# Spreading the first norm's means by DMA and subtracting them on GpSimd

## What is computed

```python
def _ln_c(v, eps=1e-06):
    m = jnp.mean(v, axis=1, keepdims=True)
    s = jnp.var(v, axis=1, keepdims=True)
    return (v - m) / jnp.sqrt(s + eps)
...
x = x + conv_ref(_ln_c(x), ...)
t = _to_tokens(x)
t = t + ffn_ref(_ln_t(t), ...)
```

## Time and profile before

| | |
|---|---|
| median of three runs | 628.01 us (627.54 to 630.71) |
| profiled execution | span 630.2 us from first to last instruction; no own time is given beside it, and of the three runs only 630.71 is not below the span |
| mean granted clock of PE | 0.916 |
| PE busy | 541.1 us, 86% of the span |
| DVE busy | 487.1 us, 77% |
| ACT busy | 436.5 us, 69% |
| POOL busy | 188.7 us, 30% |
| DMA | 73.38 MB, mean 116 GB/s |

### The profile page before, as it was taken

How to read it: one execution, slowest core, us unless ns; L and a number is a source line. 1 busy time by engine, 2 the same in 40 slices (tenths; PEclk the granted TensorE clock), 3 DMA queues, 4 the chain that set the end, 5 groups by cost and what they waited for, 6 DMA issues and landing times.

```text
span 630.2 us, 14170 instructions
## 1 busy us (share of the span) xinstructions
PE 541.1 (86%) x5732; PEld 274.7 (44%) x5732; DVE 487.1 (77%) x950; ACT 436.5 (69%) x651; POOL 188.7 (30%) x116
## 2 busy tenths in 40 slices
PE   3659999998989898998999899989898988977982
PEld 1333444444444444444444444434443433344762
DVE  5575565789888978897899779987888798799520
ACT  2455788787977796779767976897687855974110
POOL 1008362115302440235022602080308044130045
PEclk9956998999999989998999799989998999976595
DMA  8960245623661457144714453435411265520000
GB/s 193 196 152 14 101 129 158 170 80 91 189 179 62 109 156 190 57 136 134 200 70 135 133 157 113 136 101 167 134 43 61 91 182 152 160 81 5 6 16 19
DMA packets 26752, 73.38 MB, mean 116 GB/s; under 512 B 4152, under 2 KB 4152, under 8 KB 22592
## 3 DMA queue, kind: packets, MB, share of 16 engines
q1 hardware_dynamic: 25664, 71.44, 41.2%
q0 software_dynamic: 1024, 1.05, 0.6%
HBM read 38.40 MB, written 34.08 MB: 115 GB/s over the span
## 4 chain that ended last, share of the span: by engine, by line
PE 44%; DVE 28%; ACT 12%; issue 11%; DMA 2%; another core or an unknown queue 1%; POOL 0%; SPq 0%; ACTq 0%; DVEq 0%; POOLq 0%
PE st L372 10%; PE cv L383 8%; PE bc L494 6%; PE tl L400 6%; PE cv L391 5%; DVE us L949 5%; ACT junk L810 5%; DVE xs L959 5%; DVE lg L947 3%; PE tl L409 3%; DVE cnd L1041 2%; DVE top_i L1046 2%; ACT tok L775 2%; DVE us L951 2%; DMA xs<-in_x 2%
## 5 line engine op out<-in xcount | busy, mean ns | idle before, releaser
L1437 POOL TENSOR_TENSOR xs<-xs,us 128x1024 f32<-128x1024 f32 x64 | 150.7, 2376 | 360.3 <-DVE xs L959 177.4
L959 DVE SCALAR_TENSOR_TENSOR xs<-cv,vecs,xs 128x1024 f32<-128x1024 f32 x64 | 82.0, 1282 | 25.2 <-PE cv L391 24.9
L770 ACT ACTIVATE hid<-cv,b1n 128x1024 f32<-128x1024 f32 x64 | 71.3, 1115 | 39.3 <-PE cv L383 38.8
L803 ACT ACTIVATE sqc<-us 128x1024 f32<-128x1024 f32 x64 | 67.6, 1056 | 42.3 <-DVE us L949 41.6
L400 PEld LDWEIGHTS tl<-ident,xs 128*128 128x128 f32 x512 | 64.4, 196 | 56.9 <-issue 56.9
L951 DVE CUSTOM_DVE_ANT_0 us<-us,bc 128x1024 f32<-128x1024 f32 x60 | 73.0, 1216 | 19.0 <-PE bc L494 17.7
L949 DVE TENSOR_TENSOR us<-xs,bc 128x1024 f32<-128x1024 f32 x60 | 73.0, 1216 | 17.5 <-PE bc L494 17.1
L810 ACT ACTIVATE junk<-us 128x1024 bf16<-128x1024 f32 x64 | 67.5, 1055 | 20.5 <-DVE gsum L951 19.9
L372 PE MATMUL st<-xs,stat_w 128*32 128x256 f32 x1024 | 72.6, 404 | 8.9 <-DMA xs<-in_x 8.9
L400 PE MATMUL tl<-ident,xs 128*128 128x128 f32 x512 | 77.1, 296 | 1.6 <-ACT lg L785 1.6
L409 PE MATMUL tl<-xs,gcen 128*32 128x256 f32 x1024 | 71.7, 400 | 7.4 <-ACT tok L775 7.4
(11 more groups left out here) (210 smaller groups left out, 657.0 us busy)
## 6 DMA issues: line engine op xcount, KB each, us to landing
xs<-in_x SPq DMA_DIRECT2D x64, 512.0 KB, 7.0
out_rows<-tok SPq DMA_DIRECT2D x64, 512.0 KB
us<-in_e_w SPq DMA_DIRECT2D x8, 260.0 KB
xs<-in_e_w SPq DMA_DIRECT2D x8, 256.0 KB
sqc<-out_rows,idx_all POOLq DMA_INDIRECT x16
out_rows<-sqc,idx_all POOLq DMA_INDIRECT x16
vecs<-in_b SPq DMA_DIRECT2D x4, 0.2 KB, 14.0
gate_bias<-in_gate_b SPq DMA_DIRECT2D x4, 0.1 KB, 12.4
```

The source lines that it names most:

```text
L959: nc.vector.scalar_tensor_tensor(out=xu, in0=cv[:], scalar=vecs[:, 3:4], in1=xu, op0=ALU.add, op1=ALU.add).then_inc(x1_done, 1)
L1437: nc.gpsimd.tensor_tensor(xu, xu, su, ALU.add).then_inc(s_done, 1)
```

## The change

For batches 2 to 7 the first norm's mean is no longer spread by PE. DVE copies the sums of part i (pairs 0 and 1, pair 2, pair 3) into `mean_f` (which is the buffer `ta`), SP writes them to a DRAM tensor `means` in DMAs of two rows of 256 (16, 8 and 8 of them), waits until they have landed, and loads each half pair's means back into `us`, one row of 8 KB for all of 64 partitions (4, 2 and 2 DMAs). POOL then computes x - mean (centre). `xs` becomes one ring of nine pairs, so the loads move: pair 0 in step 0 of batch n - 2, pairs 1, 2, 3 in its steps 3, 5, 7. x_sums of pairs 0, 1, 2 stand in steps 4, 5, 6, of pair 3 in step 0 of the next. The squares of two units move into the batch before (`NEXT_SQUARES`), `sqc` has four units instead of three, the last square sums and ln1_rsqrt and rstd are in step 3, S jobs begin at (3, 2) and the third and fourth L job are at (2, 1) and (2, 2). In the tail, `ew2` and `eq` use the last four pairs of the ring, and the DMA scratch space is set to 4096 bytes. The core of the diff:

```diff
...
@@ -36,7 +36,8 @@
 RING = 6
 CAND = PIECES * K
 MRG = 2 * CAND + PIECES
-SQC = 3
+SQC = 4
+SLOTS = 9
...
 C_JOBS = {(0, 0): 0, (0, 1): 1, (0, 2): 2, (1, 0): 3, (2, 0): 4, (2, 1): 5, (2, 2): 6, (3, 0): 7}
-S_JOBS = {(4, 0): 0, (4, 1): 1, (4, 2): 2, (5, 0): 3, (5, 1): 4, (5, 2): 5, (6, 0): 6, (6, 1): 7}
-L_JOBS = {(1, 1): 0, (1, 2): 1, (3, 1): 2, (3, 2): 3}
+FIRST_S_JOBS = {(4, 0): 0, (4, 1): 1, (4, 2): 2, (5, 0): 3, (5, 1): 4, (5, 2): 5, (6, 0): 6, (6, 1): 7}
+S_JOBS = {(3, 2): 0, (4, 0): 1, (4, 1): 2, (4, 2): 3, (5, 0): 4, (5, 1): 5, (6, 0): 6, (6, 1): 7}
+L_JOBS = {(1, 1): 0, (1, 2): 1, (2, 1): 2, (2, 2): 3}
+LAST_L_JOBS = {(1, 1): 0, (1, 2): 1, (3, 1): 2, (3, 2): 3}
+FIRST_SQUARES = {(s, i): k for (s, i), k in C_JOBS.items()}
+SQUARES = {(0, 0): 2, (0, 1): 3, (1, 1): 4, (1, 2): 5, (2, 1): 6, (2, 2): 7}
+NEXT_SQUARES = {(7, 1): 0, (7, 2): 1}
 E_JOBS = {(7, 0): 0, (7, 2): 1}
...
     p1, tl = it + 1 < NB, 1 <= it <= NB
     jobs = {}
+    if p1 and it <= 0:
+        jobs.update({at: ("C", k) for at, k in C_JOBS.items()})
     if p1:
-        jobs.update({at: ("C", k) for at, k in C_JOBS.items()})
-        jobs.update({at: ("S", k) for at, k in S_JOBS.items()})
+        jobs.update({at: ("S", k) for at, k in (S_JOBS if it >= 1 else FIRST_S_JOBS).items()})
     if tl:
         jobs[LAST_M_JOB if it == NB - 1 else M_JOB] = ("M", it - 1)
         if it < NB:
-            jobs.update({at: ("L", k) for at, k in L_JOBS.items()})
+            jobs.update({at: ("L", k) for at, k in (L_JOBS if p1 else LAST_L_JOBS).items()})
     if it == NB - 1:
         jobs.update({at: ("E", k) for at, k in E_JOBS.items()})
     if it == NB:
...
+    return k // 2 + 1 if n == 0 else NG + k // 4 + 1
+def mean_part_count(n, i):
+    return NG + 2 + 3 * (n - 2) + i + 1
+def squares_at(it, at):
+    if it <= 0:
+        return [(it + 1, k) for k in [FIRST_SQUARES.get(at)] if k is not None] + (
+            [(it + 2, k) for k in [NEXT_SQUARES.get(at)] if k is not None] if it == 0 else [])
+    return ([(it + 1, SQUARES[at])] if it + 1 < NB and at in SQUARES else []) + (
+        [(it + 2, NEXT_SQUARES[at])] if it + 2 < NB and at in NEXT_SQUARES else [])
 def mk_metaformer_kernel(nc, x, gn_w, gn_b, w1T, b1, w2T, b2, gateT, gate_b, e_w1, e_w2, e_b2, *outs):
...
         us = [sb(f"us{i}", [P, HW]) for i in range(2)]
         lg = sb("lg", [P, RING * PIECE])
...
+        def x_col(n, u):
+            return UN * (2 * ((NG * n + u // 2) % SLOTS) + u % 2)
+        def x_unit(n, u):
+            return xs[:, x_col(n, u):x_col(n, u) + UN]
...
-            def load(b, m, slot):
+            def load(b, m):
+                col = x_col(b, 2 * m)
                 for h in range(HALVES):
-                    sp.dma_start(xs[slot][C * h:C * h + C, 2 * UN * m:2 * UN * (m + 1)], x_h[b, h, :, m, :]).then_inc(x_in[m], 16)
+                    sp.dma_start(xs[C * h:C * h + C, col:col + 2 * UN], x_h[b, h, :, m, :]).then_inc(x_in[m], 16)
+            def spread_means(n, i):
+                m0, m1 = ((0, 2), (2, 3), (3, 4))[i]
+                sp.wait_ge(mean_ready, mean_part_count(n, i))
+                if n >= 4:
+                    for m in range(m0, m1):
+                        sp.wait_ge(mean_in[m], 32 * (n - 3))
+                for c in range(4):
+                    src = mean_f[32 * c + 4 * m0:32 * c + 4 * m1, :]
+                    for m in range(m0, m1):
+                        for sub in range(2):
+                            q = 4 * (m - m0) + 2 * sub
+                            sp.dma_start(means[n % 2, m, :, c, sub, :], src[q:q + 2, :]).then_inc(mean_out, 16)
+                sp.wait_ge(mean_out, 16 * 8 * (NG * (n - 2) + m1))
+                sp.wait_ge(c_done, NU * (n - 2) + 2 * m1)
+                sp.wait_ge(s_done, NU * (n - 2) + 2 * m1)
+                for m in range(m0, m1):
+                    for h in range(HALVES):
+                        row = means[n % 2, m, h].rearrange("c s r -> (c s r)").unsqueeze(0).broadcast_to([C, 2 * UN])
+                        sp.dma_start(us[n % 2][C * h:C * h + C, 2 * UN * m:2 * UN * (m + 1)], row).then_inc(mean_in[m], 16)
...
                 sp.wait_ge(sumx_done, m + 1)
-                load(1, m, 1)
+                load(1, m)
+            sp.wait_ge(sumx_done, mean_count(1, 0))
+            load(2, 0)
             def load_weights(part):
...
             def step(it, s):
-                par, (b, u) = it % 2, (it, s - 1) if s else (it - 1, NU - 1)
+                (b, u) = (it, s - 1) if s else (it - 1, NU - 1)
+                if s == 1 and it >= 1 and it + 1 < NB:
+                    spread_means(it + 1, 2)
+                if s in (6, 7) and it + 2 < NB:
+                    spread_means(it + 2, s - 6)
                 if b >= 0:
                     store(b, u)
                 if it == NB - 1:
                     load_weights(s)
-                if s == 0 and b >= 0 and it + 1 < NB:
+                if s == 0 and b >= 0 and it + 2 < NB:
                     sp.wait_ge(grp_done, NG * it)
                     sp.wait_ge(e_done, NU * it)
-                    load(it + 1, NG - 1, 1 - par)
+                    load(it + 2, 0)
                 if it + 2 < NB and s >= 3 and s % 2 == 1:
                     sp.wait_ge(grp_done, NG * it + (s - 3) // 2 + 1)
-                    load(it + 2, (s - 3) // 2, par)
+                    load(it + 2, (s - 3) // 2 + 1)
...
-                mm = sum_group(st1[:, 0:SUB], xs[n % 2], m, NU, True)
-                if m % 2 == 1:
+                if n >= 2 and m >= 2:
+                    pe.wait_ge(mean_ready, mean_part_count(n, m - 2))
+                mm = sum_group(st1[:, 0:SUB], xs, m, x_col(n, 2 * m), True)
+                if (m >= 1) if n >= 2 else (m % 2 == 1):
                     mm.then_inc(sumx_done, 1)
             def first_x_sums(m):
                 pe.wait_ge(x_in[m], 32)
                 wait(pe, mean_ready, m)
-                sum_group(st2[:, 0:SUB], xs[0], m, NU, True).then_inc(sumx_done, 1)
...
                 if s == 0 and b >= 0:
                     x1_sums(b, b % 2, NG - 1)
-                if s == 1 and p1:
-                    xc_square_sums(n, 0)
-                if s == 2 and p1:
-                    xc_square_sums(n, 1)
+                if s in (1, 2) and it == 0:
+                    xc_square_sums(n, s - 1)
                 if s == 4:
                     x1_sums(it, par, 1)
                 if s in (3, 7):
...
-                if s in (0, 1) and p1:
+                if s in (0, 1) and it == 0:
                     x_sums(n, s + 2)
-                if s == 3 and p1:
+                if s == 0 and it >= 1 and p1:
+                    x_sums(n, 3)
+                if s == 1 and it >= 1 and p1:
+                    pe.wait_ge(mean_ready, mean_part_count(n, 2))
+                    xc_square_sums(n, 0)
+                    xc_square_sums(n, 1)
+                if s == 2 and it >= 1 and p1:
+                    xc_square_sums(n, 2)
+                if s == 3 and it == 0:
                     xc_square_sums(n, 3)
-                if s in (4, 6) and n + 1 < NB:
-                    x_sums(n + 1, s // 2 - 2)
+                if s in (4, 5, 6) and n + 1 < NB:
+                    x_sums(n + 1, s - 4)
                 if s == 4 and n + 1 >= NB:
...
+            def square_xc(n, k):
+                if n < 2:
+                    used(act, n - 1, "C", k)
+                else:
+                    act.wait_ge(xc_done, NU * (n - 2) + k + 1)
+                wait(act, sumsq_done, NG * n + k // 2 - 1)
+                nc.scalar.activation(unit(sqc, k, SQC), unit(us[n % 2], k), ACT.Square).then_inc(sqc_done, 1)
             def square_at(it, at):
+                for n, k in squares_at(it, at):
...
                 act.wait_ge(grp_done, NG * (f + 1) if f < NB - 1 else NG * (NB - 1) + 2 * (f - NB + 2))
+                if f + 2 < NB:
+                    act.wait_ge(mean_out, 16 * 8 * (NG * f + 3))
                 nc.scalar.activation(ta[:], st2[:, 0:SUB], ACT.Square).then_inc(msq_done, 1)
...
                     square_x1(b, b % 2, u)
-                if s == 4 and p1:
+                if s == 4 and it == 0:
                     ln1_rsqrt(n)
                 relu(it, par, s)
                 if s >= 1:
                     square_at(it, (s - 1, 2))
+                elif it >= 1:
+                    square_at(it - 1, (NU - 1, 2))
                 if t >= 0 and s in EXPLOG_AT:
                     explog(t, EXPLOG_AT[s])
                 if s == 6 and not p1:
                     ln2_rsqrt(NB - 1)
                 if b >= 0:
                     token_copy(b, u)
+                if s == 3 and it >= 1 and p1:
+                    ln1_rsqrt(n)
                 if s == NU - 1 and p1:
                     norm_rsqrt(n)
...
                 nc.vector.scalar_tensor_tensor(out=mean_s[:], in0=hi[:].bitcast(F32), scalar=second[:], in1=stat[:, 0:SUB],
                                                op0=ALU.mult, op1=ALU.add).then_inc(mean_ready, 1)
```

(34 more changed lines are left out.)

47 lines of the change are left out of this document (24 added, 23 removed).

## The result

The changed kernel takes 733.31 us (median of 4 runs, 732.31 to 734.14), the kernel before 628.64 (4 runs, 627.54 to 630.71): a ratio of 1.167, 95% interval 1.164 to 1.170. It is slower by 105 us, the side that was forecast (697), inside the range (640 to 750) and 36 us above the forecast. The profiled execution has a span of 731.2 us against 630.2.

The account below looks back on a forecast made before the run. PE was taken as near full, DVE close behind. Per batch, 3.0 us of compute gain against 14.5 of waiting for SP's late load gave +11.5, six times +69, so 697 us; range 640 to 750.

Parts of the forecast that it names:

- the other signs that it named: Among them: PE idle over 10 us ahead of step 0's x sums; 16 DMAs on SP in some 7 us.
- What the change takes away: Mean spreads on PE (3.5 us) and DVE subtractions (9.7 us) go; compute gains 3.0 us per batch.
- The ring's price of nothing: The larger xs ring costs nothing, since loads keep their size.
- The chain: SP's queue from mean_part(0) to the landed load of pair 3: 32.4 us, so PE waits 14.5 in step 0.
- Issue of 16 writes: SP issues part 0's 2 KB writes at 0.42 us each, 6.7 us.
- Landing and lead: On SP's queue, 1.3 us for a small write to land and 0.9 until the broadcasts move data.
- Broadcasts: Part 0's 2.1 MB move at a load pair's rate, 218 GB/s, in 9.6 us.
- Step 3: PE idles 4.2 us at its end, waiting for rstd before the first rstd spread; step 11.2 us.
- the clock's term: PE at half clock after stalls, 6 x 1.6 = +10 to +20 us, left out of the sum.
- rival 4: The stall cools PE to 1.2 instead of 2.4 GHz: 707 to 717 us, chance 0.14.
- If the load were early, these would be the next waits, at some 22 us: In step 0, the token copy waiting for store(5), and logits and x_sums behind it, would then stop PE.
- I add nothing for sharing: POOL's subtractions beside DVE's work cost 0, since its adds already lie beside L951 at undisturbed lengths.

Follow-up runs that it names:

- e2: The changed kernel with sixteen more 2 KB writes of constants in part 0 of the means, to a spare tensor nobody reads: 749.06 us, 1.191 to the kernel before.
- e5: The changed kernel with each broadcast of the means cut to 16 of its 64 partitions, the number of DMAs kept: 689.12 us, 1.096 to the kernel before.
- e3: The changed kernel with rstd's products at their old places, from (4,0) on: 698.49 us, 1.112 to the kernel before.
- e4: The kernel before with only the ring of nine pairs and the earlier loads, the first norm untouched: 628.0 us, 0.999 to the kernel before.
- e1: The changed kernel with the load of pair 3 issued ahead of part 1 of the means: 733.28 us, 1.168 to the kernel before.
- e7: The changed kernel with the edits of e1 and e3 together: 701.54 us, 1.114 to the kernel before.
- v1: The changed kernel with four-row writes, e3's edit, later squares and sums, and stores and loads between writes and broadcasts: 648.80 us, 1.036 to the kernel before.
- v2: v1 with the 2-row writes and 8 KB rows of the changed kernel: 661.83 us, 1.054 to the kernel before.
- e8: The kernel before with eight spare POOL passes per batch in batches 1 to 6, on a tile nothing else reads: 654.37 us, 1.042 to the kernel before.

## Why the prediction was right, and where it was off

**The side and the mechanism: right.** PE stands in step 0 for a load that SP issues late, released by the DMA into xs, with the DMA share at 0.60 (forecast about 0.7). Of the other signs that it named, PE's idle time ahead of these sums alone is 8.79 us and not over 10, and the 16 issues take 4.7 us and not 7. e2 (more chain, more time) shows that the spread chain costs time on the path, and e5 that its bytes are a large part of it.

**What the change takes away: there, but less.** In e3 no wait for the load or for rstd lies in steps 1 to 7, and they take 52.8 us against 55.7 before: 2.9 gained. The forecast has 54.9 for these steps, 4.8 of it waits of step 3, so without them a gain of 5.6; some 1.2 of the difference is the half clock in step 1 (below). The ring's price of nothing is e4's.

**The chain, term by term.** Sum forecast 32.4, measured 34.6 (262.31 to 296.92).
- Issue of 16 writes: 6.7 forecast, 4.7 measured (0.29 each, not 0.42).
- Landing and lead: 2.2 forecast, 4.1 measured (267.04, the end of the issues, to 271.2, where the broadcasts move). The load of pair 2 isn't the reason: its data had moved before the last write was issued, and from 268 to 271 the DMA engines do nothing (share 0.00 above). It is the landing itself, 2.9 us from the end of the issues instead of 1.3. The section of the Trainium skill from which the prediction takes a fixed 2.0 us ("DMA: Bandwidth & Descriptors", Anatomy of one DMA) describes DMAs that GpSimd issues; here SP issues them, and it waits 2.9 us for part 0 and 1.6 for part 2.
- Broadcasts: 9.6 and 9.9. The load's rate was the right row.
- Store, writes and their landing: 1.9 and 2.9. Then part 1's broadcasts, store and load: 12.0 and 12.9.

That the first two errors cancel (-2.0 and +1.9) is luck; the others leave the chain 2.2 us longer than forecast. PE stands 4.29 + 8.79 = 13.1 us in step 0, forecast 14.5. That part of it is a wait for relu was named in the forecast (relu "some 5 us late").

**Step 3: right.** 4.2 us of idle forecast, 3.92 measured, step 10.7 against 11.2. But the price of the edit was larger than the wait: e3 gives 5.8 per batch.

**What fell short is the clock's term, which the sum left out.** The period is 81.6, 5.2 above the forecast. Blocks at half clock account for most of it: the x sums, conv1 and tokens behind the load take 5.4 us (296.92 to 302.31) instead of 3.1, and tokens, x sums and conv1 behind rstd take 4.6 (325.01 to 329.63) instead of 3.1, together 3.8 per batch, 23 us in all. A third stretch, 282.58 to 288.1, is hidden under the wait for the load. So rival 4 was true on top of the forecast: after each wait PE ran at 1.2 instead of 2.4 GHz, and its upper end would have given 717. By the Trainium skill ("TensorE: Matmul & The Clock Gate", What's actually happening) the throttled state is the default; the trace agrees with 0.50 behind all three waits, though behind the third only from about 326 on, 1.3 us after PE went on. The reason for leaving it out, that the old dip in step 5 may go, came true (step 5 takes 7.3 us against 8.0), but was too weak beside new waits that were larger than any in the kernel before. Of the other 1.4 us per batch, 1.3 are in step 0: the chain is 2.2 longer and starts 0.9 earlier (12.8 us ahead of step 0, forecast 11.9). What is left of the other steps' differences, between -0.5 and +0.5 each, nearly cancels.

**"If the load were early, these would be the next waits, at some 22 us": the order right, the room wrong.** That sentence leaves several us to gain. e1 and e7 show none: the deadlines of load, relu, token copy and last squares all hang on one queue, and an edit that moves one transfer forward moves the others back. Only v1 and v2, which give each a new place and move the squares later as well, bring the period down by moving transfers, to 69 and 71.

**"I add nothing for sharing": wrong in its reason.** The row it rests on is L951, one of whose inputs is in PSUM; e8 shows that such an operation isn't held, but that a SCALAR_TENSOR_TENSOR with both inputs in SBUF is. DVE's groups in one batch of the kernel after (the third is a cast with one input, held as well):
```profile
L1123 DVE SCALAR_TENSOR_TENSOR rstd_s<-hi,second,tb 128x256 fp32r<-128x256 f32 x1 | 2.4, 2443 | 0.0
L1145 DVE SCALAR_TENSOR_TENSOR cnd<-top_i,rowoff,top_hi 128x32 f32<-128x32 uint32 x1 | 2.3, 2298 | 0.0
L1193 DVE CAST idx_all<-pxf 128x2 uint32<-128x2 f32 x1 | 1.8, 1768 | 0.0
```
The same three take 0.49, 0.25 and 0.17 in the kernel before. The 5.6 us are DVE time; how much of it is on the path wasn't separated. Two of the three (at 277.74 and 291.29) fall into step 0, where PE stands for the load anyway; the third (at 349.05) is in step 7, which takes 6.9 us instead of the 6.4 of before.

**What stays open.** Why v1 is still 20 us above before is argued from its waits, not shown one by one. By the table 3.8 of its 4.1 us per batch lie in step 3, where the store behind broadcasts and the late subtraction stop PE for 4.3 us. Of the held DVE operations only cnd is left in v1 (2.3 us, in step 7); rstd_s and idx_all have their old 0.48 and 0.17. No version with the spread by DMA beat the kernel before.
